# The product with v between the second and third score pair, the projection or FFN block behind the fourth, in a fused attention and FFN kernel

## What is computed

```python
q, k, v = proj(Wq, bq), proj(Wk, bk), proj(Wv, bv)          # 16 heads of 16
q = rope(q) * 16 ** -0.5;  k = rope(k)
attn = softmax(einsum('bhsd,bhtd->bhst', q, k), axis=-1)
out  = einsum('bhst,bhtd->bhsd', attn, v) @ Wo.T + bo
x = layernorm(x + out)
h = relu(x @ ternary(W1).T + b1)                            # 256 -> 1024
x = layernorm(x + h @ ternary(W2).T + b2)                   # 1024 -> 256
```

## Time and profile before

| | |
|---|---|
| median of 3 runs | 3391.64 us (3390.05 to 3392.06) |
| profiled execution | 3384.53 us |
| its span, first to last instruction | 3382.7 us |
| PE busy | 3261.7 us, 96% |
| DVE busy | 2985.4 us, 88% |
| ACT busy | 2512.8 us, 74% |
| POOL busy | 2168.1 us, 64% |
| mean granted TensorE clock | 0.982 |

### The profile page before, as it was taken

The page is one execution under the profiler, slowest core; times in us unless marked ns, Lnnn a source line. Parts: engine busy times, 40 slices in busy tenths (PEclk is TensorE's granted clock), DMA queues, the critical chain, the costliest instruction groups (busy, mean ns, idle before and its releaser), DMA issues.

```text
span 3382.7 us, 81458 instructions
## 1 busy us (share of the span) xinstructions
PE 3261.7 (96%) x30726; PEld 1784.6 (53%) x30726; DVE 2985.4 (88%) x5670; ACT 2512.8 (74%) x4884; POOL 2168.1 (64%) x2479
## 2 busy tenths in 40 slices
PE   6999999999999999999999999999999999999975
PEld 4434555555555555555555555555555555544444
DVE  7888999999999999999999999999999999999921
ACT  2777777777777777777777777777777777777740
POOL 3535766766776676676677667667766766734456
PEclk7999999999999999999999999999999999999987
DMA  6444454355345445534444543553454454344110
GB/s 186 103 94 98 98 114 104 92 116 116 96 100 117 99 97 114 113 92 110 114 98 101 114 105 91 115 118 92 104 116 100 97 113 108 91 89 82 35 43 26
DMA packets 310792, 339.09 MB, mean 100 GB/s; under 512 B 77056, under 2 KB 259200, under 8 KB 310400
## 3 DMA queue, kind: packets, MB, share of 16 engines
q1 hardware_dynamic: 310400, 333.89, 43.2%
HBM read 193.27 MB, written 140.51 MB: 99 GB/s over the span
## 4 chain that ended last, share of the span: by engine, by line
PE 94%; POOL 2%; DVE 1%; ACT 1%; DMA 1%; issue 1%; SPq 0%; POOLq 0%; DVEq 0%; ACTq 0%
PE ob L716 30%; PE sc L699 29%; PE job L571 25%; PE ms L688 9%; ACT prob L821 1%; POOL hid_r L1188 1%; DVE mxp L1069 1%; PE ms L571 0%; PE job L624 0%; PE ob L571 0%; POOL ka L1280 0%; PE sc L571 0%; DVE hid L1000 0%; DVE w_sb L1105 0%; POOL hid_r L1186 0%
## 5 line engine op out<-in xcount | busy, mean ns | idle before, releaser
L952 DVE TENSOR_REDUCE mxp<-ms 128x1 f32<-128x512 f32 x4064 | 2620.9, 682 | 246.1 <-PE ms L688 200.0
L821 ACT ACTIVATE prob<-sc 128x512 f32<-128x512 f32 x4096 | 2224.8, 597 | 687.1 <-PE sc L699 662.5
L699 PE MATMUL sc<-qa,ka 50*128 50x512 f32 x4096 | 1545.4, 443 | 27.5 <-ACT prob L821 27.5
L688 PE MATMUL ms<-ka,qa 48*128 48x512 f32 x4064 | 1539.5, 445 | 0.4 <-DVE mxp L952 0.4
L699 PEld LDWEIGHTS sc<-qa,ka 50*128 50x128 f32 x4096 | 683.2, 184 | 1119.0 <-ACT prob L821 970.5
L716 PE MATMUL ob<-prob,v_sb 128*17 128x512 f32 x8192 | 1078.2, 598 | 0.3
L688 PEld LDWEIGHTS ms<-ka,qa 48*128 48x128 f32 x4064 | 679.1, 184 | 6.6 <-DVE mxp L952 4.2
L1167 POOL TENSOR_TENSOR ve<-mv,eps_sb 128x2 f32<-128x2 f32 x128 | 25.2, 197 | 517.3 <-DVE mv L979 517.3
L1188 POOL TENSOR_TENSOR hid_r<-hid,hid_r 128x512 fp32r<-128x512 f32 x256 | 328.7, 1284 | 20.5
L571 PEld LDWEIGHTS job<-h_t,w_sb 64*128 64x128 f32 x3840 | 259.7, 185 | 23.3
L716 PEld LDWEIGHTS ob<-prob,v_sb 128*17 128x17 f32 x8192 | 136.0, 95 | 256.1 <-issue 255.2
(11 more groups left out here) (135 smaller groups left out, 2817.6 us busy)
## 6 DMA issues: line engine op xcount, KB each, us to landing
qk_parts<-parts SPq DMA_DIRECT2D x124, 512.0 KB, 4.3
ka<-qk_parts SPq DMA_DIRECT2D x378, 128.0 KB, 4.6
qa<-qk_parts SPq DMA_DIRECT2D x378, 128.0 KB, 7.3
attention<-at_st SPq DMA_DIRECT2D x128, 256.0 KB, 3.0
v_ones<-v_st SPq DMA_DIRECT2D x64, 272.0 KB, 2.4
v_sb<-v_ones SPq DMA_DIRECT2D x64, 272.0 KB, 8.6
xn<-x SPq DMA_DIRECT2D x64, 256.0 KB, 4.8
ao<-attention SPq DMA_DIRECT2D x128, 128.0 KB
```

The source lines that it names most:

```text
L688: nc.tensor.matmul(ms[upto(b, g, NS1, at) % MS_BANKS][:, :], operand(qa, b, g, j, ROWS)[:, qt * P:(qt + 1) * P], operand(ka, b, g, j, ROWS ...
L699: nc.tensor.matmul(sc[upto(b, g, HG * STEPS, n) % SC_BANKS][:, :], operand(ka, b, g, j, ROWS + MROWS)[:, tt * P:(tt + 1) * P], operand(qa, ...
L821: nc.scalar.activation(prob[st_ % 2][:, j, :], sc[upto(b, g, HG * STEPS, n) % SC_BANKS][:, :], ACT.Exp).then_inc(s["exp_done"], 1)
L952: nc.vector.reduce_max(mxp[(b * G + g) % 2][:, kh, j * TT + qt:j * TT + qt + 1], ms[upto(b, g, NS1, at) % MS_BANKS][:, :], AX.X).then_inc( ...
```

## The change

1. PE: in a step the product with v stands always between the second and the third score tile; the job stands behind the fourth.
2. Its consumers follow half a step later. ACT takes a job's results at the start of the next step and behind its second exponential, and copies `ob` in steps 0 and 8 (before 1 and 9). DVE takes the hidden tile behind its last maximum of the step and its first of the next. The key half of e1 and o1 moves from DVE to ACT. `FIRST_NORM` ends at (5, 0), before at (4, 2).
3. `OWN_STEPS` is 1, before 4, so that combining and turning of the maxima fall in steps 1 and 9, before 4 and 12. Unit 0 keeps its own table: 20 tiles in its first 4 steps as before, then 5 a step, before 4.
4. SP: `move_maxima(b, g, 1)` goes ahead of `tail_in`, and `tail_out` to behind `move_maxima` of the next unit.
5. POOL: `split_maxima(b, g, 1)` and `sum_x` go to the front of a unit; `finish_second_norm` goes from the front to behind the last `split_hidden`; its inputs (`SECOND_NORM`) are made in steps 8 and 10, before 0 to 2.

The core of the diff:

```diff
@@ -47,7 +47,9 @@
 EPS = 1e-5
 Q_SCALE = HD ** -0.5
 NS1 = HG * TT * 2
-OWN_STEPS = 4
+OWN_STEPS = 1
+FIRST_STEPS = 4
+FIRST_RATE = 5
 HALF_TILES = NS1 // QH
 IN_WAIT = 12
@@ -56,14 +58,17 @@
-SECOND_SPLIT_STEP = 5
+SECOND_SPLIT_STEP = 6
 ...
-FIRST_NORM = {(1, 1): "sum 0", (1, 2): "sum 1", (2, 2): "stats 0", (4, 0): "stats 1", (4, 2): "moments 0"}
-SECOND_SUMS = {(15, 1): "sum 0", (15, 2): "sum 1"}
-SECOND_NORM = {(0, 1): "stats 0", (0, 3): "stats 1", (2, 0): "moments 0"}
+FIRST_NORM = {(1, 3): "sum 0", (2, 0): "sum 1", (3, 2): "stats 0", (4, 2): "stats 1", (5, 0): "moments 0"}
+SECOND_SUMS = {(15, 3): "sum 0"}
+SECOND_NORM = {(0, 0): "sum 1", (8, 1): "stats 0", (10, 1): "stats 1", (10, 2): "moments 0"}
 ...
+FIRST_MAXIMA_AT = {(FIRST_STEPS, 0): "combine 1", (FIRST_STEPS, 1): "turn 1", (FIRST_STEPS + 7, 0): "combine 0", (FIRST_STEPS + 7, 1): "turn 0"}
+FIRST_SEEN = 7 * FIRST_RATE
@@ -95,9 +100,9 @@
 def maximum_tiles(b, g, n, last):
     own = 4 * OWN_STEPS
+    if b == g == 0:
+        return FIRST_TILES[n]
     if n < own:
-        if b == g == 0:
-            return FIRST_TILES[n]
         return [(b, g, NS1 - own + n, NS1 - own + n)]
     if last and g == G - 1:
         return []
@@ -106,14 +111,24 @@
-    begin, at, parts = HALF_TILES + IN_WAIT, HALF_TILES + IN_WAIT, []
-    own = 4 * OWN_STEPS
+    own, parts = 4 * FIRST_STEPS, []
+    begin = at = HALF_TILES + IN_WAIT
 ...
+    at = 0
+    for step in range(STEPS - FIRST_STEPS):
+        block = range(step * FIRST_RATE, (step + 1) * FIRST_RATE)
+        upper, lower = [i for i in block if i % 4 < 2], [i for i in block if i % 4 >= 2]
+        for some in (upper[:1], upper[1:], lower[:1], lower[1:]):
+            tiles = []
+            for i in some:
+                tiles.append((0, 1, at, i))
+                at += 1
+            parts.append(tiles)
     return parts
@@ -477,11 +492,9 @@
                     store_attention(b + (g - 1) // G, (g - 1) % G, 1)
                 if not (last and g == G - 1):
                     load_v(b + (g + 1) // G, (g + 1) % G)
-                if tail if g else tail_before:
-                    tail_out(b - 1 + (g - 1) // G, (g - 1) % G)
+                move_maxima(b, g, 1)
                 if prepared(b, g)[0] >= 0:
                     tail_in(*prepared(b, g))
-                move_maxima(b, g, 1)
                 if len(proj) > 1:
                     proj_out(*proj[0])
                 for at in projected_next(b, g):
@@ -491,6 +504,8 @@
                     attention_in(*prepared(b, g))
                 if not (last and g == G - 1):
                     move_maxima(b + (g + 1) // G, (g + 1) % G, 0)
+                if tail if g else tail_before:
+                    tail_out(b - 1 + (g - 1) // G, (g - 1) % G)
                 for at in proj[-1:]:
                     proj_out(*at)
@@ -747,10 +762,9 @@
                         for j in range(HG):
                             scores(b, g, st_, j, tiles[j])
                             if j == 1:
-                                for job_ in jobs:
-                                    free = run(job_, free)
-                            if j == (3 if jobs else 1):
                                 weigh_before(b, g, st_, first)
+                        for job_ in jobs:
+                            free = run(job_, free)
             pe.wait_ge(s["ones_set"], 1)
             pe.wait_ge(s["weights_low"], 2)
@@ -882,22 +899,27 @@
+                elif name == "t4":
+                    tail_job(*at, name, tiles=(1,))
+                elif name in ("e1", "o1"):
+                    proj_job(*at, name, (1,))
 ...
                     for st_ in range(STEPS):
-                        if st_ == TT + 1:
-                            take_outputs(b, g, 0)
-                        if st_ == 1 and not (first and g == 0):
-                            take_outputs(b + (g - 1) // G, (g - 1) % G, 1)
+                        done = jobs_at(b, g, st_ - 1, tail) if st_ else []
+                        for job_ in done:
+                            finish(job_)
                         exps(b, g, st_, 0)
                         exps(b, g, st_, 1)
-                        for job_ in jobs_at(b, g, st_, tail):
-                            finish(job_)
+                        for job_ in done:
+                            finish_rest(job_)
+                        if st_ == TT:
+                            take_outputs(b, g, 0)
+                        if st_ == 0 and not (first and g == 0):
+                            take_outputs(b + (g - 1) // G, (g - 1) % G, 1)
                         exps(b, g, st_, 2)
                         exps(b, g, st_, 3)
-                        for job_ in jobs_at(b, g, st_, tail):
-                            finish_rest(job_)
                         if st_ == SECOND_SPLIT_STEP:
                             for at in projected(b, g)[1:]:
                                 split_x(*at)
@@ -985,13 +1008,6 @@
-                elif name in ("e1", "o1"):
-                    eo = "eo".index(name[0])
 ...
-                    nc.vector.tensor_scalar((ev_sb, od_sb)[eo][:, 1, :], job[1][:, 0:TQ], bqk_sb[:, 1, eo:eo + 1], None, ALU.add
-                                            ).then_inc(s[full + "_taken"], 1)
@@ -1047,19 +1063,23 @@
-                            chain = maxima_of(b, g, MAXIMA_AT.get((st_, part)))
+                            chain = maxima_of(b, g, (MAXIMA_AT if b or g else FIRST_MAXIMA_AT).get((st_, part)))
 ...
-                            for stage, at, name in jobs_at(b, g, st_, tail):
-                                if stage == "proj" and part == 1:
-                                    take_key_half(*at, name)
-                                elif name in ("f1", "f3") and part in (1, 2):
-                                    p = part - 1
-                                    take_hidden(*at, int(name[1]) - 1 + p, job[1][:, p * TQ:(p + 1) * TQ])
+                            if part == 3:
+                                for stage, at, name in jobs_at(b, g, st_, tail):
+                                    if name == "v1":
+                                        take_key_half(*at, name)
+                                    elif name in ("f1", "f3"):
+                                        take_hidden(*at, int(name[1]) - 1, job[1][:, 0:TQ])
+                            if part == 0 and st_:
+                                for stage, at, name in jobs_at(b, g, st_ - 1, tail):
+                                    if name in ("f1", "f3"):
+                                        take_hidden(*at, int(name[1]), job[1][:, TQ:2 * TQ])
@@ -1225,11 +1245,14 @@
             def unit(b, g, tail, tail_before, last):
                 proj = projected(b, g)
-                if tail if g else tail_before:
-                    finish_second_norm(b - 1 + (g - 1) // G, (g - 1) % G)
+                if b or g:
+                    split_maxima(b, g, 1)
+                if prepared(b, g)[0] >= 0:
+                    sum_x(*prepared(b, g))
                 for at in proj[:1]:
                     rotate_even(pool, nc.gpsimd, *at)
-                split_maxima(b, g, 1)
+                if not (b or g):
+                    split_maxima(b, g, 1)
                 if tail:
                     finish_first_norm(b - 1, g)
                     sum_h1(b - 1, g)
@@ -1243,19 +1266,16 @@
+                if not (last and g == G - 1):
+                    split_maxima(b + (g + 1) // G, (g + 1) % G, 0)
+                for at in proj[1:]:
                     rotate_odd(pool, nc.gpsimd, *at)
-                    split_maxima(b + (g + 1) // G, (g + 1) % G, 0)
                     add_products(pool, nc.gpsimd, *at)
                 if tail:
-                    split_hidden(b - 1, g, 0)
-                    split_hidden(b - 1, g, 1)
-                if prepared(b, g)[0] >= 0:
-                    sum_x(*prepared(b, g))
-                if tail:
-                    split_hidden(b - 1, g, 2)
-                    split_hidden(b - 1, g, 3)
-                if not (last and g == G - 1) and len(proj) < 2:
-                    split_maxima(b + (g + 1) // G, (g + 1) % G, 0)
+                    for n in range(FT // 2):
+                        split_hidden(b - 1, g, n)
+                if tail if g else tail_before:
+                    finish_second_norm(b - 1 + (g - 1) // G, (g - 1) % G)
```

More of the change, by code:

```diff
@@ L812, in finish @@
                 stage, at, name = job_
-                {"proj": proj_job, "tail": tail_job}[stage](*at, name)
+                if stage == "proj":
+                    proj_job(*at, name)
+                else:
+                    tail_job(*at, name, tiles=(0,))
             def exps(b, g, st_, j):
@@ L864, in take_hidden, with tail_job @@
                                      ).then_inc(s["f_even_taken"], 1)
-            def tail_job(b, g, name, end=False):
+            def tail_job(b, g, name, end=False, tiles=(0, 1)):
                 banks = banks_of(name, end)
@@ L872, in tail_job @@
```

(12 more changed lines are left out.)

## The result

The changed kernel takes **3899.28 us** (median of 4 runs, 3887.51 to 3904.58) against 3391.14 us (4 runs, 3390.05 to 3392.06): a ratio of 1.1498, 95% interval 1.1483 to 1.1514. It is 15% slower. The profiled execution took 3894.94 us, its span is 3893.1, and the mean granted clock 0.928 (0.982 before).

The account below looks back on a forecast made before the run. PE's sequence was taken to set the time. To the profiled 3384.5 us it added 367 + 26 + 10 of standstill, 108 for the clock and 3 for unit 0, giving 3898.5, so a median of 3906 us, range 3740 to 4000.

Parts of the forecast that it names:

- The order on PE: PE's sequence in each step: the new order is worth 0, a gain at most 0.3 us a unit.
- DVE and ACT: Two evacuations a unit moving from DVE to ACT cost nothing, covered by ACT's 10.5 us of idle time.
- Unit 0: Five maxima tiles a step instead of 4 from step 4 on: +3 us once, bounds 0 and 8.
- Landing of v: v's load lands 14.2 us into the unit before; later `parts` stores add 1.9 us, bounds 0 and 2.7.
- Hold by the stores: The maxima's loads, waiting for their stores in the full queue, issue 0.8 us after v lands, bounds 0 and 2.
- PE's standstill: PE waits at t4 for `h1`: 6.8 us in 54 units, +367; every fourth unit +26; units 58 to 61 +10.
- The clock: PE's granted clock halves after each long idle time: 2.0 us in 54 units, +108 us, bounds 0 and 135.
- The sum: Whole kernel: 3384.5 us profiled plus the terms gives 3898.5, and 7.1 more for the median gives 3906 us.
- The small store overtakes: Rival: on the queue the 16 KB maxima stores skip the backlog; stall 3.2 us, median 3594, 3700 with clock drop; chance 0.12.
- xn early enough: Rival: xn lands by 13.6 us, so PE has no wait; 0.3 us a unit won, 3372 us; chance 0.05.
- The chain feeds on itself: Rival: behind the stall f0 or t3 waits too, `parts` goes ever later; 1 us more a unit, 3960; chance 0.1.

Follow-up runs that it names:

- e1: Not a run: a piece of work in the kernel whose key half the change moves from DVE to ACT; POOL's rotation of the even rows waits for it.
- xb-late: The changed kernel with `xb<-xn` on POOL moved back between the hidden tiles, SP's order staying the changed one: 3402.74 us, 1.0035.
- xn-first: The changed kernel with SP's load of xn ahead of the unit's loads of q and k: 3402.91 us, 1.0043.
- order-alone kernel: The kernel before with only points 1 and 2 of the change; maxima's steps, second norm, SP and POOL as before: 3410.8 us, 1.0067.
- the filled stall: The changed kernel with 46 pairs of matmuls, results unread, on PE ahead of t4's wait for `h1`: 3835.34 us, 1.1317.
- the kernel with the DMA and `xb` alone: The kernel before with only xn loaded behind the maxima's stores on SP, and maxima split and `xb` first on POOL: 4083.84 us, 1.2052.

## Why the prediction was right

3906 us was forecast and 3899 measured, with the mechanism, its place and most of the sizes as written. Point by point:

- **The order on PE: nothing.** Right for the change as a whole: 49.64 and 49.65 us a unit in the xb-late and xn-first kernels, 49.60 before. The order-alone kernel shows a condition that I had not stated: the half step makes ACT's piece of e1 late for POOL's rotation, and with the split of the maxima between rotation and first norm, as before, the 0.2 us to spare at t4 are gone and 0.3 us a unit are lost.
- **DVE and ACT: nothing.** In keeping with the 49.64 us a unit, but no run gives e1 and o1 back to DVE. The kernel that gives DVE two other pieces has a unit 0.24 us longer.
- **Unit 0.** +3 forecast, +3.3 in the trace (56.27 against 52.95 us), and 0.6 more in unit 1.
- **Landing of v:** 14.2 + 1.9 = 16.1 forecast, 16.3 measured; every fourth unit 18.0 against a forecast of 18.1 to 18.5. `parts` went out 2.05 us before the unit's end, forecast 2.0. The size fits, the path to it only in part: SP also took longer over the loads (last section), and v itself landed 8.6 us behind its issue and not 9.1.
- **Hold by the stores:** 0.8 forecast, 0.26 measured in unit 28, 0.35 in the mean of units 4 to 57. The value from unit 2 was too high; why is open. In 6 of these 54 units the maxima's loads go out ahead of v's landing, by up to 0.73 us, so the order of landing is not strict. The rest of the chain: loads 0.60 (0.6), xn 2.8 (2.9), `xb` to `h1` 7.0 (7.1). xn landed at 19.9 and not 20.4, `h1` at 26.9 and not 27.5.
- **PE's standstill:** 367 + 26 + 10 = 403 forecast, 386.8 measured in 59 waits. The start of t4 came as forecast: against the 2.1 us into step 6 that I had taken it is 393 us late over units 4 to 57, and 367 + 26 = 393 were forecast (6.5 in unit 28, so more in every fourth unit). But PE is ready only at 2.36 us, since the second pair of score tiles waits for ACT's exponentials; 0.26 x 59 = 15 are no standstill, and step 7 gives them back (2.82 us in the kernels without a stall).
- **The clock:** +108 forecast; 251 / 2 = 126 by the time at half clock, of which the filled stall wins 81 back. The half clock lasts 4.65 us behind t4's start in the mean, where I had taken 4.5 and counted 4.0 of it.
- **The sum:** 386.8 + 126 + 3.9 is 517; the two executions differ by 3894.94 - 3384.5 = 510, so some 7 must come back in other steps, which I did not trace. The clock was 18 too low and the standstill 16 too high: part of the closeness is luck. So is the last unit, whose clock did not fall in this execution.

The rivals. **The small store overtakes** is refuted by SP's timeline: the wait of 8.4 us ends 0.26 behind v. What the Trainium skill, "DMA: Bandwidth & Descriptors", section on queues, rings and completion order, says of descriptors taken in ring order on each DMA engine agrees with that. What it says of completion out of the order of issue is seen too, but small: by up to 0.73 us for the stores in the change, and by up to 2.1 us for xn in the xn-first kernel. The kernel with xn ahead of the stores made the rival's world by hand, and measured 3722 where the prediction had 3700 for it with a drop of the clock: my first choice there, no drop, would have been wrong by 128. **xn early enough** was not to be had by the queue, but the xn-first kernel shows it: 49.65 us a unit, so the 0.3 us above the pure steps that this rival hoped for were not won. **The chain feeds on itself** did not happen: step 8 takes 3.27 us, no more than the 3.32 of the xb-late kernel, the later ones have their old length, and the units hardly grow (58.74 us in the mean of units 8 to 31, 58.89 in 32 to 55). What I did not foresee is the last unit's clock; in the profiled execution of the change itself it did not fall there.

## What to carry to other kernels

Before a step is moved up in an in-order engine's list, ask when its own input lands, by the queue that loads it, and what stands behind it: `xb` was free where it stood and cost 500 us ahead of the rotation and the norm, while its input was equally late in both places. On a queue with 9 us of backlog the 16 KB round trip cost the backlog and not its own size (8.9 us from store to load in the mean, 2.6 before), and what is issued behind the wait pays too. A long standstill of PE is to be priced with the clock behind it, here between 81 and 126 of the 510 us.

## What the runs showed of the hardware that I had not expected

- The granted clock fell to 0.50 for 20.5 us in the last unit of the xb-late kernel, with PE busy for 19.73 of them by the profile. Ahead of it PE had no idle time over 0.45 us in that unit, but was busy for only 5.90 of the last 7.10 us. The stretch has few matmuls (78), no maxima and no jobs. In unit 28 of that kernel the clock stayed at 1.00, with 486 matmuls in 49.64 us. Sixteen more matmuls, whose results go nowhere, brought the mean of the same stretch to 0.83. Why two of six runs of the same kernel kept the clock is open.
- Idle times of the same length do not always end alike: in the kernel with xn ahead of the stores one of 2.52 us was followed by a drop, and one of 2.98 us by none. In the changed kernel all of 4.67 us or more were, none of up to 1.69.
- In unit 28 of the change SP took 4.16 us to issue the six loads of `ka` that took it 2.64 before, with the queue running later; in units 8 to 55 the means are 3.91 and 2.83. Here the stores of `parts`, 512 KB each, go out right ahead of these loads. In the kernel with the DMA and `xb` alone, where they go out 4.7 us before the unit's end as before, the mean is 2.84. So the slow issue goes with the later `parts`; no run shows whether a full queue is what slows the issue.
